# Dense attention on one core: row maxima computed 28 instead of 26 score tiles ahead

## The chip, the cores and the metric

The kernel runs on one core of a Trainium2 chip. The metric is the device time of one execution in microseconds (us); lower is better. The engines are TensorE (PE; its weight loads, PEld, are listed apart), VectorE (DVE), ScalarE (ACT), GpSimd (POOL) and SyncE (SP), which issues the DMAs. Each engine works through its own instructions in order; semaphores tie the engines together.

## What is computed

`x` is (2, 2048, 256). After a first layer norm, two branches read it: a dense attention branch with 16 heads of width 16, and a local attention and feed-forward branch of two layers. The result is `x + s * silu(f)`. The change touches only the dense branch:

```python
qkv = einsum('bnd,ed->bne', x, W_qkv)            # 16 heads of width 16
attn = einsum('bhnd,bhmd->bhnm', q, k) * hd**-0.5
attn = attn + spatial_bias                       # nonzero for tokens 1..256 only
attn = softmax(attn, axis=-1)
out = einsum('bhnm,bhmd->bhnd', attn, v)
out = out @ W_proj.T + b_proj + layernorm(x)
```

## The kernel before

The kernel has three phases: projections and the splitting of q and k into bf16 parts (to about 111 us), the dense attention (111 to 1472 us), and the window branch (to the end). Only the second phase is touched.

**Tiles and groups.** For each of the 16 heads `h` the scores are computed in 128 steps (`STEPS`). A step is one tile of 128 keys by 512 queries. Sixteen steps make a group (`KB` = 16): one batch row and one chunk of 512 queries; a head has 8 groups, groups 0 to 3 for batch row 0 and 4 to 7 for batch row 1. Before a group's first score can be computed, the largest score of each of its 512 queries must be known, because it is subtracted inside the score matmul through two extra rows of `q_aug` (the shift). So the same products are computed once more beforehand, with queries on the partitions (`max_tile`, L1460: four matmuls of 32 columns side by side). Two such tiles are a pair, and eight pairs cover a group: pairs 0 to 7 are group 0, pairs 48 to 55 are group 6. The maxima run `LEAD` tiles ahead of the scores, across the border between heads.

**PE.** Its order is written out in the loop over `turns()` (from L1503). In each step: `scores_to_exp` (L1475), in eight of sixteen steps also `weighted` (probabilities times values, L1492; `PV_PLAN` says where: steps 0, 2, 4, 6, 7, 10, 12, 14 of a group), and in each odd step the two tiles of pair `(step + LEAD) // 2`. `scores_to_exp` waits at a group's first step until the shift rows are stored (`shift_saved`). A pair's tiles go to PSUM banks 4 and 5 or 6 and 7 in turn, so the matmuls of pair t wait until DVE has read pair t-2 (`smax_read`).

**DVE** reads each pair with one reduction (`max_pair`, L1145). In `turns()` order it also does the transposition of a group's shift (`turn_shift`, L1165). It stands behind the first pair of the next group (L1190 to L1193): the shift of group 5 behind pair 48. It waits there for `shift_ready`, and all later reductions are queued behind it.

**POOL** works in the order of `serve_head`. For each group, `split_max` forms four row maxima (L641, each waits for its two pairs), rounds them to bf16 (L645), subtracts (L647, which releases `shift_ready`), waits for DVE's transposition and copies its result into `q_aug` with four instructions (L657). Two things stand between groups. `apply_bias` (L635) multiplies three probability tiles of group 0 and of group 4. `copy_values` (L625) loads the values of a batch row; ahead of the row maxima of group 5 it loads batch row 0 of the next head, for which it waits until the last `weighted` of group 3, at step 71, is done. The last head has no such copy.

**ACT** takes the exponential of each score tile (L919) and stores the sums of each group (L902). **SP** loads `q_aug` and `k_aug` of batch row 0 of the next head after the scores of step 63, and stores the sums.

**The start.** Before step 0, PE computes `LEAD` tiles. DVE reads the first eight pairs, forms the first shift, reads `LEAD // 2 - 8` more pairs (L1182), then sets one row of the bias table (L1185), which releases POOL's first `apply_bias`. The `weighted` of step 10 waits for it (`bias_done`). **The end.** Pair 63 of head 15 is the last, so the last steps have no maxima.

Of the kernel before, what the change touches and what calls it, by code (L numbers as in the profile page):

```python
# [32 lines left out]
KB = N // P  # L33
# [4 lines left out]
SHIFT_ROWS = 2  # L38
CT = 32
AUG = TERM_ROWS + SHIFT_ROWS  # L40
LEAD = KB + 10
TURN = 32
TURNS = P // TURN
PRING = 16
# [43 lines left out]
def build(nc, x, wqkT, wvT, wpT, b_proj, gamma, beta, centers, centersT, wqkv, qk_gain, qk_gain_swapped, rotary,  # L88
# [9 lines left out]
    with ExitStack() as top:  # L98
# [951 lines left out]
        def _(dve):  # L1050
# [88 lines left out]
            def max_pair(h, t):  # L1139

                group, q, half = t // (PAIRS // GROUPS), (t // 2) % QC, t % 2
                if t % (PAIRS // GROUPS) == 0 and h * GROUPS + group >= 2:
                    dve.wait_ge(max_step, 2 * (h * GROUPS + group - 2) + 1)
                dve.wait_ge(smax_ready, h * PAIRS + (t + 1))
                nc.vector.tensor_reduce(pair_max[:, group % 2, q, half:half + 1],  # L1145
                                        banks[:, 4 + 2 * (t % 2):6 + 2 * (t % 2), :],
                                        AX.XY, ALU.max).then_inc(smax_read, 1)
# [33 lines left out]
            nc.vector.tensor_tensor(dmax[:, 4:5], dmax[:, 5:6], dmax[:, 3:4], ALU.mult).then_inc(dist_scale, 1)  # L1181
            for t in range(PAIRS // GROUPS, LEAD // 2):  # L1182
                max_pair(0, t)
            dve.wait_ge(dist_exp, 1)
            nc.vector.memset(bias_exp[0:1, 0, :], 1.0).then_inc(bias_ready, 1)  # L1185
            for h, steps, ends in turns():
                for step in steps:
                    tile = step + LEAD
                    if tile % 2 == 0 or ends and tile > STEPS + 1:
# [222 lines left out]
        def _(pe):  # L1412
# [41 lines left out]
            def max_tile(before, t):  # L1454

                pair, b, q, kq = t // 2, (t // (QC * KB)) % B, (t // (N // BANK)) % KB, t % (N // BANK)
                if t % 2 == 0:
                    pe.wait_ge(smax_read, before + (pair + 1))
                for m in range(0, P, CT):
                    last = nc.tensor.matmul(banks[m:m + CT, 4 + t % 4, :],  # L1460
                                            q_aug[0:TERM_ROWS, b, q * P + m:q * P + m + CT],
                                            k_aug[0:TERM_ROWS, b, kq * BANK:(kq + 1) * BANK], start=True, stop=True)
                if t % 2 == 1:
                    last.then_inc(smax_ready, 1)
# [15 lines left out]
            def weighted(h, group, first, half):  # L1480

                b = group // QC
                if first == 0 and half == 0:
                    pe.wait_ge(acc_saved, h * GROUPS + (group + 1))
                    pe.wait_ge(v_copied, h * 2 + (3 + b))
                    if group % QC == 0:
                        pe.wait_ge(bias_done, h * 6 + (b * 3 + 3))
                if half == 0:
                    pe.wait_ge(prob_ready, h * STEPS + (group * KB + first + 5))
                cols = slice(half * HALF, (half + 1) * HALF)  # L1490
                for g in range(4):
                    last = nc.tensor.matmul(banks[CT * g:CT * g + VW, 3, cols], v_cur[:, b, first + g, :],  # L1492
                                            probs[:, (group * KB + first + g) % PRING, cols],
                                            start=(first == 0 and half == 0), stop=(first == KB - 4),
                                            skip_group_check=True)
                last.then_inc(pv_done, 1)

            nc.tensor.sem_inc(pv_done, 1)
            pe.wait_ge(aug_loaded[0], AUG_LOADS)
            for t in range(LEAD):  # L1500
                max_tile(0, t)
            pe.wait_ge(minus_set, 1)
            for h, steps, ends in turns():  # L1503
                for step in steps:
# [5 lines left out]
                    if group + ago >= 0:  # L1510
                        weighted(h, group + ago, first, half)
                    pair = (step + LEAD) // 2
                    if step % 2 == 1 and not (ends and pair >= PAIRS):
# [318 lines left out]
```

## Time and profile before

| | value |
|---|---|
| median of 3 runs | 2928.17 us (2927.76 to 2928.51) |
| the profiled execution's own time | 2928.38 us |
| its span, first to last instruction | 2926.6 us |
| mean granted TensorE clock | 0.993 |
| PE busy | 2883.0 us (99%) |
| DVE busy | 2336.9 us (80%) |
| ACT busy | 2222.5 us (76%) |
| POOL busy | 1265.3 us (43%) |
| DVE reductions of pairs, L1145 | 1024 of 1214 ns |

The busy time of PE is taken from modelled ends of matmuls, so 99% says that PE nearly always had work, not that it ran at its peak. The idle time before an instruction and what ended it stand in square brackets in the timeline rows. A line number in a row is that of the kernel.

### The profile page before, as it was taken

Reading aid. Unit: us, or ns where it says so; the run is one execution under the profiler, and the core shown is the slowest. Engines: PE = TensorE matmul, PEld = TensorE weight load, DVE = VectorE, ACT = ScalarE, POOL = GpSimd, SP = SyncE. Lnnn points to the kernel's source line nnn. Section 1 sums busy time; section 2 is a strip of 40 time slices with the busy share of each in tenths; the row PEclk is TensorE's granted clock in tenths of the full one; section 3 lists DMA queues with packets and bytes.
Section 4 is the critical chain, followed back from the end, with each engine's and each line's share of the span. In section 5 each row is a group of like instructions: output and inputs, shape, how many; then the busy total and the mean of one; then the engine's idle time right before and its main releaser. Section 6 shows DMA issues by size and latency. Waiting matters only on the chain.

```text
span 2926.6 us, 107289 instructions
## 1 busy us (share of the span) xinstructions
PE 2883.0 (99%) x44160; PEld 2025.9 (69%) x44160; DVE 2336.9 (80%) x4346; ACT 2222.5 (76%) x4251; POOL 1265.3 (43%) x2348
## 2 busy tenths in 40 slices
PE   8899999999999999999999999999999999999998
PEld 4467666655667755767657777777777777777776
DVE  7899999999999999999856776777677677767765
ACT  4599999999999999999966666666666666666664
POOL 5432333333333323332345455555555554555554
PEclk9899999999999999999999999999999999999999
DMA  7631111111111111111121111111111111111110
GB/s 233 211 115 41 49 49 45 43 49 49 41 46 49 49 39 48 49 49 39 44 65 45 36 31 37 40 47 44 30 37 33 47 45 36 31 38 39 47 43 5
DMA packets 157393, 154.78 MB, mean 53 GB/s; under 512 B 17794, under 2 KB 130946, under 8 KB 156930
## 3 DMA queue, kind: packets, MB, share of 16 engines
q1 hardware_dynamic: 156930, 148.15, 16.3%
q8 instruction: 346, 5.67, 0.8%
q14 instruction: 117, 0.96, 0.1%
HBM read 89.37 MB, written 58.72 MB: 51 GB/s over the span
## 4 chain that ended last, share of the span: by engine, by line
PE 95%; DVE 2%; POOL 1%; ACT 1%; issue 1%; SPq 0%; DMA 0%; POOLq 0%; DVEq 0%; ACTq 0%
PE banks L1534 29%; PE banks L1492 15%; PE banks L1460 15%; PE banks L1475 14%; PE banks L1601 4%; PE banks L1549 4%; PE banks L1639 4%; PE banks L1568 3%; PE banks L1616 2%; PE banks L1429 1%; PE banks L1626 1%; DVE pair_max L1145 1%; PE banks L1447 1%; POOL row_max L641 1%; PE banks L1714 0%
## 5 line engine op out<-in xcount | busy, mean ns | idle before, releaser
L1145 DVE TENSOR_REDUCE pair_max<-banks 128x1 f32<-128x1024 f32 x1024 | 1212.4, 1214 | 106.9 <-PE banks L1460 76.4
L919 ACT ACTIVATE probs<-banks 128x512 f32<-128x512 f32 x2048 | 1186.5, 599 | 99.3 <-PE banks L1475 13.1
L1475 PE MATMUL banks<-q_aug,k_aug 98*32 98x512 bf16 x8192 | 845.7, 381 | 0.2
L1460 PE MATMUL banks<-k_aug,q_aug 96*32 96x512 bf16 x8192 | 663.0, 383 | 8.5 <-DVE pair_max L1145 3.8
L1492 PE MATMUL banks<-probs,v_cur 128*32 128x256 f32 x8192 | 655.7, 379 | 2.1 <-POOL probs L635 2.0
L1492 PEld LDWEIGHTS banks<-probs,v_cur 128*32 128x32 f32 x8192 | 319.3, 111 | 144.1 <-issue 2.4
L1460 PEld LDWEIGHTS banks<-k_aug,q_aug 96*32 96x32 bf16 x8192 | 276.8, 97 | 188.2 <-DVE pair_max L1145 60.2
L641 POOL TENSOR_SCALAR row_max<-pair_max 128x1 f32<-128x1 f32 x508 | 139.6, 278 | 611.0 <-DVE pair_max L1145 603.1
L1475 PEld LDWEIGHTS banks<-q_aug,k_aug 98*32 98x32 bf16 x8192 | 287.3, 95 | 150.4 <-ACT probs L919 4.7
L1534 PEld LDWEIGHTS banks<-hnT,w_sb 128*64 128x64 f32 (+1 forms) x5632 | 308.5, 137 | 25.1 <-ACT hnT L998 25.1
L1534 PE MATMUL banks<-hnT,w_sb 128*64 128x128 f32 (+1 forms) x5632 | 323.9, 275 | 0.9 <-ACT hnT L998 0.9
L730 POOL TENSOR_TENSOR norms<-norms,half_power 128x4 f32<-128x4 f32 (+1 forms) x192 | 232.4, 1220 | 181.1 <-DVE norms L1254 181.1
L939 ACT ACTIVATE masked<-banks 128x512 f32<-128x512 f32 x128 | 76.5, 598 | 302.1 <-DVE masked L1222 267.4
L1266 DVE CUSTOM_DVE_ANT_0 masked<-banks,mask,norms 128x256 f32<-128x256 f32 x512 | 212.3, 479 | 43.9 <-PE banks L1601 43.9
L1534 PE MATMUL banks<-wqkv_sb,xT 128*64 128x512 f32 x1024 | 246.2, 602 | 0.0
L1245 DVE TENSOR_REDUCE norms<-masked 128x8 f32<-128x512 f32 x128 | 87.1, 681 | 170.5 <-ACT masked L939 170.5
L657 POOL COPY q_aug<-shift_rows 2x128 bf16<-2x128 bf16 x512 | 146.0, 285 | 161.8 <-DVE shift_rows L1165 138.4
L1534 PE MATMUL banks<-pT,w_sb 128*64 128x128 f32 x3072 | 181.7, 274 | 0.0
L1325 DVE SCALAR_TENSOR_TENSOR pT<-banks,b_sb,pT 128x128 f32<-128x128 f32 (+1 forms) x384 | 113.2, 343 | 74.0 <-PE banks L1534 72.6
L1534 PEld LDWEIGHTS banks<-pT,w_sb 128*64 128x64 f32 x3072 | 169.2, 137 | 3.8
L983 ACT COPY pT<-banks 128x1024 f32<-128x1024 f32 x128 | 123.3, 1015 | 60.9 <-PE banks L1616 60.9
L757 POOL TENSOR_TENSOR oT<-row_sums,one 128x512 f32<-128x512 f32 x64 | 66.5, 1040 | 208.1 <-DVE row_sums L1284 208.1
(143 smaller groups left out, 4020.5 us busy)
## 6 DMA issues: line engine op xcount, KB each, us to landing
acc_scratch<-acc_sb SPq DMA_DIRECT2D x128, 256.0 KB, 2.5
heads_win<-acc_scratch SPq DMA_DIRECT2D x512, 64.0 KB
q_aug<-q_parts SPq DMA_DIRECT2D x192, 64.0 KB, 2.2
k_aug<-k_parts SPq DMA_DIRECT2D x192, 64.0 KB, 2.2
q_parts<-parts SPq DMA_DIRECT2D x16, 384.0 KB, 3.1
k_parts<-parts SPq DMA_DIRECT2D x16, 384.0 KB, 4.1
x_in<-in_x SPq DMA_DIRECT2D x10, 512.0 KB, 4.9
xT_scratch<-xnT SPq DMA_DIRECT2D x8, 512.0 KB, 5.4
```

Source lines behind the costliest of these rows:

```text
L641: last = nc.gpsimd.tensor_scalar(row_max[:, q:q + 1], pair_max[:, group % 2, q, 0:1], pair_max[:, group % 2, q, 1:2], None, ALU.max)
L657: nc.gpsimd.tensor_copy(cols[:, :, g, :], shift_rows[g * TURN:g * TURN + SHIFT_ROWS]).then_inc(shift_saved, 1)
L730: nc.gpsimd.tensor_tensor(norm, norm, half_power[:, 0:last - first], ALU.pow).then_inc(inv_norms, 1)
L919: nc.scalar.activation(probs[:, step % PRING, :], banks[:, ring(h, step), :], ACT.Exp, scale=SCALE).then_inc(prob_ready, 1)
L983: nc.scalar.copy(pT[:, b, first:first + LH // 2].rearrange("p h c (r t) -> p r (h c) t", r=2), banks[:, lanes(b) + first // 2:lanes(b) + f ...
L1145: nc.vector.tensor_reduce(pair_max[:, group % 2, q, half:half + 1], banks[:, 4 + 2 * (t % 2):6 + 2 * (t % 2), :], AX.XY, ALU.max).then_inc ...
L1266: last = nc.vector.tensor_tensor_reduce(masked[:, b, p, :], banks[:, lanes(b) + p // 2, col:col + 2 * WINDOW], mask[:], norms[:, b, head_a ...
L1460: last = nc.tensor.matmul(banks[m:m + CT, 4 + t % 4, :], q_aug[0:TERM_ROWS, b, q * P + m:q * P + m + CT], k_aug[0:TERM_ROWS, b, kq * BANK: ...
L1475: last = nc.tensor.matmul(banks[m:m + CT, ring(h, step), :], k_aug[0:AUG, b, kb * P + m:kb * P + m + CT], q_aug[0:AUG, b, qc * CHUNK:(qc + ...
L1492: last = nc.tensor.matmul(banks[CT * g:CT * g + VW, 3, cols], v_cur[:, b, first + g, :], probs[:, (group * KB + first + g) % PRING, cols], ...
L1534: last = nc.tensor.matmul(out[first:first + size], stationary[:, first:first + size], moving, start=start, stop=stop)
L1549: last = nc.tensor.matmul(out, tokens, weights, start=(f == 0), stop=(f == 1))
```

## The change

One constant is raised:

```diff
-LEAD = KB + 10
+LEAD = KB + 12
```

`LEAD` is 28 instead of 26. PE computes 28 tiles before step 0, and each later pair two steps earlier: the first pair of a group stood in step 7 of a group and now stands in step 5. DVE, POOL, ACT and SP keep their order, but for one pair that DVE reads ahead of the row of the bias table. The last pair of the last head moves from step 101 to step 99.

On DVE, at the start of the second phase, between the first shift's arithmetic and the second shift's transposition:

```order
-L1145 TENSOR_REDUCE pair_max<-banks 128x1 f32<-128x1024 f32 x5
+L1145 TENSOR_REDUCE pair_max<-banks 128x1 f32<-128x1024 f32 x6
 L1185 MEMSET bias_exp 1x256
-L1145 TENSOR_REDUCE pair_max<-banks 128x1 f32<-128x1024 f32 x4
+L1145 TENSOR_REDUCE pair_max<-banks 128x1 f32<-128x1024 f32 x3
```

One reduction moved ahead of the memset; the transposition still follows the ninth of them.

On PE, in head 0, steps 70 to 73 before. L1475 is a step's score tile, L1492 is `weighted`, L1460 a pair of maxima; the second L1492 is the last of group 3, for which POOL's copy of the values waits, and the first L1460 is pair 48:

```order
L1475 MATMUL banks<-q_aug,k_aug 32x512 x4
L1492 MATMUL banks<-probs,v_cur 32x256 x4
L1475 MATMUL banks<-q_aug,k_aug 32x512 x4
L1492 MATMUL banks<-probs,v_cur 32x256 x4
L1460 MATMUL banks<-k_aug,q_aug 32x512 x8
L1475 MATMUL banks<-q_aug,k_aug 32x512 x8
L1460 MATMUL banks<-k_aug,q_aug 32x512 x8
```

The same place in the changed kernel, one row earlier, so that pair 48 is in it, which is the first L1460 and belongs to step 69:

```order
L1460 MATMUL banks<-k_aug,q_aug 32x512 x8
L1475 MATMUL banks<-q_aug,k_aug 32x512 x4
L1492 MATMUL banks<-probs,v_cur 32x256 x4
L1475 MATMUL banks<-q_aug,k_aug 32x512 x4
L1492 MATMUL banks<-probs,v_cur 32x256 x4
L1460 MATMUL banks<-k_aug,q_aug 32x512 x8
L1475 MATMUL banks<-q_aug,k_aug 32x512 x8
L1460 MATMUL banks<-k_aug,q_aug 32x512 x8
```

Pair 48 moved two steps up. The `weighted` of step 71 stood ahead of pair 48 and now stands behind it.

## Rows read from the trace of the kernel before

**Rows 1.** Stretches view: length, busy us of PE, PEld, DVE, ACT, POOL, then clock.

```profile
160.00:1455.00 1295.00, 1293.43 (x23711) 856.27 (x23706) 1188.54 (x1112) 1205.01 (x2099) 403.81 (x1356) 1.00 0.16 50
```

**Rows 2.** DVE timeline, ordinary group: start us, us, what, [idle before <-releaser].

```profile
702.53 1.23 DVE L1145 TENSOR_REDUCE pair_max<-banks 128x1 f32<-128x1024 f32 x1 [0.59 <-PE banks L1460]
...
703.89 8.50 DVE L1145 TENSOR_REDUCE pair_max<-banks 128x1 f32<-128x1024 f32 x7
712.98 1.23 DVE L1145 TENSOR_REDUCE pair_max<-banks 128x1 f32<-128x1024 f32 x1 [0.59 <-PE banks L1460]
```

**Rows 3.** PE timeline, head 7: pair 50, weighted of step 76, pair 51.

```profile
766.64 0.72 PE L1460 MATMUL banks<-k_aug,q_aug 96*32 96x512 bf16 x8
...
767.30 0.72 PE L1492 MATMUL banks<-probs,v_cur 128*32 128x256 f32 x8
...
768.36 0.62 PE L1460 MATMUL banks<-k_aug,q_aug 96*32 96x512 bf16 x8
```

**Rows 4.** Waits between engines, 160 to 1440 us: us in total, times, longest.

```profile
PEld banks L1460 <- DVE pair_max L1145: 44.3, 219, 0.6
POOL v_cur L625 <- PE banks L1492: 33.2, 15, 2.2
...
DVE shift_rows L1165 <- POOL shift L647: 4.9, 15, 0.3
```

**Rows 5.** POOL timeline: copy of values, then the shift of group 5.

```profile
764.87 0.40 POOL L625 COPY v_cur<-v_all 128x256 f32<-128x256 f32 x1 [2.24 <-PE banks L1492]
765.25 1.03 POOL L641 TENSOR_SCALAR row_max<-pair_max 128x1 f32<-128x1 f32 x4
...
766.63 0.21 POOL L647 TENSOR_TENSOR shift<-row_max,shift 128x4 bf16<-128x4 f32 x1
```

**Rows 6.** DVE timeline there: pair 48, transposition, pairs 49 to 55.

```profile
765.32 1.22 DVE L1145 TENSOR_REDUCE pair_max<-banks 128x1 f32<-128x1024 f32 x1 [0.58 <-PE banks L1460]
766.88 0.31 DVE L1165 STREAM_TRANSPOSE shift_rows<-shift 128x128 bf16<-128x128 bf16 x1 [0.34 <-POOL shift L647]
767.12 8.35 DVE L1145 TENSOR_REDUCE pair_max<-banks 128x1 f32<-128x1024 f32 x7
```

**Rows 7.** POOL timeline: end of an ordinary split_max, group 6.

```profile
775.56 0.28 POOL L641 TENSOR_SCALAR row_max<-pair_max 128x1 f32<-128x1 f32 x1 [2.33 <-DVE pair_max L1145]
...
776.20 0.21 POOL L647 TENSOR_TENSOR shift<-row_max,shift 128x4 bf16<-128x4 f32 x1
```

**Rows 8.** POOL timeline, group 0 of a head: apply_bias, last row maximum.

```profile
718.65 2.12 POOL L635 TENSOR_TENSOR probs<-probs,bias_exp 128x256 f32<-128x256 f32 x3 [2.85 <-ACT probs L919]
...
722.94 0.28 POOL L641 TENSOR_SCALAR row_max<-pair_max 128x1 f32<-128x1 f32 x1 [1.41 <-DVE pair_max L1145]
```

**Rows 9.** SP timeline: issue of six loads of q_aug, next head.

```profile
759.33 4.06 SPq L433 DMA_DIRECT2D q_aug<-q_parts  x6
```

**Rows 10.** DVE timeline at the start: five pairs, the bias table row.

```profile
122.19 5.97 DVE L1145 TENSOR_REDUCE pair_max<-banks 128x1 f32<-128x1024 f32 x5
128.16 0.27 DVE L1185 MEMSET bias_exp<- 1x256 f32 x1
```

**Rows 11.** POOL timeline at the start: an all-reduce, then apply_bias.

```profile
116.67 0.38 POOL L619 PARTITION_ALL_REDUCE dmax<-dmax  x1 [5.93 <-issue]
...
133.82 2.08 POOL L635 TENSOR_TENSOR probs<-probs,bias_exp 128x256 f32<-128x256 f32 x3 [10.56 <-ACT probs L919]
```

**Rows 12.** PE timeline at the start: step 10 weighted, pair 19.

```profile
136.16 0.64 PE L1492 MATMUL banks<-probs,v_cur 128*32 128x256 f32 x8 [1.98 <-POOL probs L635]
...
139.03 0.61 PE L1460 MATMUL banks<-k_aug,q_aug 96*32 96x512 bf16 x8 [0.72 <-DVE pair_max L1145]
```

**Rows 13.** ACT timeline, end of the phase, no maxima on PE.

```profile
1457.93 7.97 ACT L919 ACTIVATE probs<-banks 128x512 f32<-128x512 f32 x16
```

**Rows 14.** Stretches view: the start after step 7, and a stretch behind the phase.

```profile
132.00:142.00 10.00, 7.30 (x132) 3.40 (x124) 6.80 (x7) 6.26 (x12) 5.63 (x16) 1.00 0.01 2
...
1480.30:1483.50 3.20, 3.20 (x12) 1.04 (x12) 0.71 (x2) 1.07 (x2) 1.99 (x2) 0.50 0.60 155
```

## The prediction

> **What bounds the kernel now.** I read the stretches view first. From 160 to 1455 us PE is busy for 1293.4 of 1295 us at full clock; DVE has 1188.5 and ACT 1205.0 us of work [rows 1]. Then DVE's timeline of an ordinary group: the same reduction comes back after 712.98 - 702.53 = 10.45 us [rows 2]. In a group PE has 16 score tiles and 16 tiles of maxima of four matmuls each, and eight `weighted`, which the trace shows as eight matmuls each, as many as a pair [rows 3]. So a group is 16 + 16 + 2 x 8 = 48 slots of 0.218 us, one behind the other. PE's own work is the bound, and neither its amount nor the length of a slot changes. A gain can only come from a stall of PE that goes, a loss only from one that comes.
>
> The stalls are few. The waits view has one that belongs to a place in each head: 15 times POOL's copy of values waits for PE (33.2 us), and 15 times DVE's transposition waits for POOL's shift, 4.9 us in all [rows 4]. It is the shift of group 5, in every head but the last.
>
> **That place, before.** POOL's copy waits for the `weighted` of step 71 and starts at 764.87. Four row maxima, the cast and the subtraction follow, and the shift is ready at 766.63 + 0.21 = 766.84 [rows 5]. DVE had read pair 48 from 765.32 on, then stood 0.34 us, transposed at 766.88 and began with pair 49 at 767.12 [rows 6]. PE may start pair 51 only when pair 49 has been read: it did at 768.36, which is 1.24 us behind the start of that reduction [rows 3]. Without a wait, pair 51 would have come six slots behind pair 50: 766.64 + 6 x 0.218 = 767.95 [rows 3]. PE lost 0.41 us here; 4.9 us over 15 heads, 0.33 each, say the same for the others [rows 4].
>
> **The same place, after.** Nothing that sets the moment of the shift moves: the copy waits for the same `weighted` of step 71, at the same place of PE's order of scores. So shift at 766.84, transposition at 766.88, pair 49's reduction at 767.12, pair 51 not before 768.36 (in the clock of before). What moves is pair 51: it belongs to step 75 instead of 77. Two scores and a `weighted` (1 + 1 + 2 slots) no longer stand ahead of it, nor does pair 48, which is now done before the `weighted` of step 71 (2 slots). Counted from that `weighted`, PE comes to it six slots earlier, at 766.64. It stands 768.36 - 766.64 = **1.72 us**, with the scores of step 76 and all else queued behind. The loss grows by 6 x 0.218 = 1.31 us for each head. DVE waits with nothing to do from the end of pair 48's reduction, about 765.32 - 0.58 = 764.74 [rows 6], to 766.88.
>
> Is it given back, or does more follow? PE has no reserve to give back [rows 1]. Behind the stall DVE reads pairs 49 to 55 in 8.35 us; with the last one 1.22 long this is (8.35 - 1.22) / 6 = 1.19 us for each [rows 6]. Pair 52 then may start at 767.12 + 1.19 + 1.24 = 769.55, and PE reaches it at 768.36 + 1.31 = 769.67. No second stall, by 0.12 us only; after that DVE gains 0.12 us with each pair. Sum: 15 x 1.31 = **+19.6 us**.
>
> **The ordinary groups.** The shift is ready at 776.20 + 0.21 = 776.41 [rows 7], 0.94 us behind the end of the group's last reduction at 767.12 + 8.35 = 775.47 [rows 6]. After the change one reduction of 1.22 us stands between that end and the transposition, so the shift is there about 0.28 us early, and DVE doesn't wait. The transposition (0.2 us of DVE: 703.89 against 702.53 + 1.23, with the overlap of about 0.1) falls into the 0.59 us in which DVE waits for PE anyway [rows 2]. That gives DVE slack and PE nothing: 0. Were the cover of 0.28 us gone, DVE would wait by what is missing, and PE would stand only from some 0.2 us on, the slack that is left of the 0.59.
>
> In group 0 of a head `apply_bias` stands ahead of the row maxima. It ends at 718.65 + 2.12 = 720.77; four maxima, cast and subtraction take 766.84 - 765.25 = 1.59 us [rows 5], so the shift is ready at 722.36. DVE would start its transposition when the reduction of the pair of step 5 is done, close to 722.9, since that is what POOL's last row maximum waited for at 722.94 [rows 8]. Cover: 0.5 us. At 0. Should it be gone by some tenths, PE still has a slot or two before it needs the pair.
>
> The first maxima of the next head need its `q_aug` at step 101 instead of 103. The six loads are issued in 4.06 us [rows 9], the six of `k_aug` behind them, from step 64 on; 37 steps of 0.65 us are 24 us. At 0.
>
> **The start.** One more pair is read ahead of the bias table's row. DVE reads these at 5.97 / 5 = 1.19 us [rows 10], so the row is set at 129.4 instead of 128.2. POOL's first `apply_bias` started at 133.82, 5.4 us behind the end of that memset at 128.43, though step 0's probabilities were there long before [rows 10, 11]. There is a like gap ahead of the all-reduce: 5.93 us with no releaser [rows 11]. If the 5.4 us run from the semaphore on, `apply_bias` moves by 1.2 us and with it the `weighted` of step 10, on which PE already stands 1.98 us [rows 12]; if they run from somewhere earlier, it stays at 133.82. I take +1.2, because the gap has the length of the all-reduce's; the other end is 0.
>
> The Trainium skill, "GPSIMD Engine Reference", section "Instruction dispatch", says that the first call into freshly loaded code pays about 6 us after its wait, with no visible instruction. The rows agree with 5.9 and 5.4 us. By that rule the term would be the +1.2 already taken from the rows.
>
> PE's longer lead of about 1.2 us (one more pair at DVE's rate) is not added: PE is waiting at step 10 in either case. From there on pair 19 is held by the second shift at 139.03 [rows 12], as before, plus the 1.2; it is now issued in step 11, so the scores run two steps behind it.
>
> **The end.** For that, two more steps have no maxima. These run at ACT's pace there, 7.97 / 16 = 0.50 us a step [rows 13]: **+1.0 us**. The pairs themselves are no more than before.
>
> **Sum:** 19.6 + 1.2 + 0 + 1.0 = 21.8 us. The profiled execution took 2928.38 us for a span of 2926.6; its new span would be 2948.4 and its time 2950.2. The median lies 0.2 us lower: 2928.17 + 21.8 = **2950.0 us**.
>
> **Rivals.**
> 1. *The clock falls at each new stall.* PE now stands 1.7 us in the middle of dense work, 15 times. A stretch of 3.2 us behind the phase was granted half the clock, after PE had idled [rows 14]. If each stall brought one such stretch, half of 3.2 us of PE's time would be lost each time: 15 x 1.6 = 24 us more, 2974. Against it: at the start PE stood 1.98 and 0.72 us within 4 us [rows 12], and 132 to 142 us was granted 1.00 [rows 14]. Chance 0.05. The Trainium skill, "TensorE: Matmul & The Clock Gate", section "HAM oscillation — how this bites in real kernels", tells of a kernel whose PE waited for each tile and fell to the lower rate every time; that rule would give this rival's time, and the start of this trace does not bear it out for a stall of this length.
> 2. *The stall does not grow.* DVE waits longer, but PE is not held, for instance since the reads of pairs 49 and 50 catch up before PE comes. Then only start and end are left, +2.2 us: 2930.4. For it: 0.41 us is all that PE loses now. Against it: PE was held at exactly that pair, and needs it six slots earlier. Chance 0.05.
> 3. *Faster: PE's waits for DVE in ordinary groups are real time.* PE's weight loads wait 44.3 us for DVE, 219 times [rows 4], near two in each group; the transposition's move starts the reduction of a group's second pair 0.2 us earlier and could end them. It decides from 21.8 / 127 = 0.17 us a group on. With all 44.3 us gone: 2928.2 + 21.8 - 44.3 = 2905.7. Against it: a group lasts 48 even slots with those waits in it, so they lie under the matmuls ahead. Chance 0.02.
>
> That the change does not do what it says is no rival: the order shows pair 48 ahead of the `weighted` of step 71.
>
> **How the numbers follow.** Forecast 0.86, rival 1 0.05, rival 2 0.05, rival 3 0.02, something unseen 0.02. The range takes in the unknown of the start (-1.2), a stall by 0.1 to 0.3 us off in each head (up to 4.5), and a second short stall at pair 52, whose cover is 0.12 us: 2943 to 2957. About 0.2% (6 us) is what a measurement of this kernel can tell from no change. Faster 0.02, same 0.05, slower 0.93.
>
> **What would show it.** Right: DVE's transposition waits for POOL's shift 15 times for some 2.1 us, over 30 us in the waits view; PE stands ahead of pair 51 about 1.7 us in each head, in step 75; an ordinary group still lasts 10.45 us, with DVE's idle time ahead of the pair of step 7 down from 0.59 to near 0.4; `apply_bias` first starts near 135.0; the phase ends near 1494. Wrong: ordinary groups that change in length, a granted clock below 1 in the phase after 140 us, or the transposition waiting in ordinary groups too, which would cost some tenths of a microsecond 112 times.

## The result and the profile after

The median is 2949.82 us (2949.60 to 2952.09, 6 runs) against 2928.25 us (2927.76 to 2928.90, 6 runs): 21.6 us or 0.75% slower. The ratio is 1.0075, 95% interval 1.0062 to 1.0088. The forecast was 2950.0. The profiled execution took 2949.7 us for a span of 2947.9, at a mean granted clock of 0.993 as before.

The stretches view of the changed kernel (length, busy us of PE, PEld, DVE, ACT, POOL, then clock), to be held against [rows 1]; below it, three stretches of the start:

```profile
160.00:1455.00 1295.00, 1274.05 (x23356) 843.46 (x23352) 1192.38 (x1095) 1187.66 (x2068) 397.50 (x1335) 1.00 0.16 49
132.60:139.40 6.80, 3.89 (x68) 1.45 (x64) 3.40 (x4) 3.31 (x7) 5.11 (x15) 1.00 0.01 2
139.50:142.80 3.30, 3.30 (x40) 1.29 (x34) 2.50 (x3) 1.79 (x3) 0.44 (x2) 0.50 0.00 0
142.90:160.00 17.10, 17.10 (x324) 9.06 (x316) 15.20 (x16) 15.62 (x28) 3.98 (x16) 1.00 0.05 19
```

PE's busy time in the same 1295 us fell from 1293.4 to 1274.1. Its idle time, 1.6 us before, is 21 us now. At the start, behind two stands of PE, the clock was granted at half rate (1.2 GHz instead of 2.4) from 139.4 to 142.8 us; the trace of the kernel before has full rate there [rows 14].

The waits view, 160 to 1440 us, answers [rows 4]:

```profile
POOL v_cur L625 <- PE banks L1492: 33.2, 15, 2.2
DVE shift_rows L1165 <- POOL shift L647: 31.0, 15, 2.1
PEld banks L1460 <- DVE pair_max L1145: 28.4, 15, 1.9
ACT probs L919 <- PE banks L1475: 24.6, 15, 1.7
PE banks L1460 <- DVE pair_max L1145: 20.9, 15, 1.4
```

POOL's wait for the `weighted` of step 71 is unchanged, 33.2 us in 15. DVE's wait for the shift went from 4.9 to 31.0 us, again 15 times and so in no ordinary group. PE's weight loads wait for DVE 15 times instead of 219. The place itself in head 7, in the timelines of POOL, DVE and PE; they answer [rows 5], [rows 6] and [rows 3]:

```profile
776.64 0.40 POOL L625 COPY v_cur<-v_all 128x256 f32<-128x256 f32 x1 [2.20 <-PE banks L1492]
...
778.41 0.21 POOL L647 TENSOR_TENSOR shift<-row_max,shift 128x4 bf16<-128x4 f32 x1
```

```profile
775.37 1.23 DVE L1145 TENSOR_REDUCE pair_max<-banks 128x1 f32<-128x1024 f32 x1
778.65 0.31 DVE L1165 STREAM_TRANSPOSE shift_rows<-shift 128x128 bf16<-128x128 bf16 x1 [2.06 <-POOL shift L647]
778.89 8.37 DVE L1145 TENSOR_REDUCE pair_max<-banks 128x1 f32<-128x1024 f32 x7
```

```profile
778.31 0.43 PE L1475 MATMUL banks<-q_aug,k_aug 98*32 98x512 bf16 x4
780.13 0.61 PE L1460 MATMUL banks<-k_aug,q_aug 96*32 96x512 bf16 x8 [1.39 <-DVE pair_max L1145]
```

The chain from the copy to the shift has kept its length, 778.62 - 776.64 = 1.98 us. Pair 48 is read from 775.37 on, before the copy that the shift waits for has begun; DVE then stands 2.06 us. Pair 49 begins to be read at 778.89 and PE starts pair 51 at 780.13, 1.24 us later as before. A slot behind the score at 778.31 would have been 778.53: a stall of 1.60 us. The 1.39 us in the row are less, because modelled ends of matmuls reach into the gap.

An ordinary group, timeline of DVE, answers [rows 2]:

```profile
808.33 1.23 DVE L1145 TENSOR_REDUCE pair_max<-banks 128x1 f32<-128x1024 f32 x1 [0.15 <-PE banks L1460]
809.47 0.30 DVE L1165 STREAM_TRANSPOSE shift_rows<-shift 128x128 bf16<-128x128 bf16 x1
810.00 2.36 DVE L1145 TENSOR_REDUCE pair_max<-banks 128x1 f32<-128x1024 f32 x2 [0.23 <-PE banks L1460]
```

The transposition waits for nothing. Of the 0.59 us for which DVE waited for PE once a group, 0.15 are left ahead of the pair of step 5 and 0.23 ahead of that of step 7. The start, timelines of POOL and PE, answers [rows 11] and [rows 12]; the end, timeline of ACT, answers [rows 13]:

```profile
133.48 2.09 POOL L635 TENSOR_TENSOR probs<-probs,bias_exp 128x256 f32<-128x256 f32 x3 [10.53 <-ACT probs L919]
```

```profile
135.83 0.64 PE L1492 MATMUL banks<-probs,v_cur 128*32 128x256 f32 x8 [0.81 <-ACT probs L919]
...
138.71 0.62 PE L1460 MATMUL banks<-k_aug,q_aug 96*32 96x512 bf16 x8 [2.02 <-DVE pair_max L1145]
```

```profile
1479.44 7.99 ACT L919 ACTIVATE probs<-banks 128x512 f32<-128x512 f32 x16
```

In this execution the second phase began 0.30 us earlier (first maxima at 110.37 instead of 110.67). With that taken off, `apply_bias` and pair 19 stand where they stood before, though the bias table's row was set 1.1 us later (done at 129.26 instead of 128.43).

### The profile page after: what moved, and what is told of

Same layout as the page of the kernel before. It is cut to its first block, busy times and chain, and to the rows that moved or that the text cites. A ratio compares the mean times of both kernels' runs of the same rounds, so it can differ in the third digit from the quotient of the medians.

```text
span 2947.9 us, 107289 instructions
## 1 busy us (share of the span) xinstructions
PE 2884.4 (98%) x44160; PEld 2028.4 (69%) x44160; DVE 2362.8 (80%) x4346; ACT 2222.8 (75%) x4251; POOL 1267.9 (43%) x2348
## 4 chain that ended last, share of the span: by engine, by line
PE 93%; DVE 4%; POOL 1%; issue 1%; ACT 1%; SPq 0%; DMA 0%; POOLq 0%; DVEq 0%; ACTq 0%
PE banks L1534 29%; PE banks L1492 15%; PE banks L1460 15%; PE banks L1475 15%; PE banks L1601 4%; PE banks L1549 4%; PE banks L1639 4%; PE banks L1568 3%; PE banks L1616 2%; DVE pair_max L1145 1%; PE banks L1626 1%; DVE xn L1091 1%; POOL row_max L641 1%; DVE xn L1081 0%; DVE rest L1098 0%
## 5 line engine op out<-in xcount | busy, mean ns | idle before, releaser
L1145 DVE TENSOR_REDUCE pair_max<-banks 128x1 f32<-128x1024 f32 x1024 | 1226.5, 1221 | 79.5 <-PE banks L1460 40.6
L1475 PE MATMUL banks<-q_aug,k_aug 98*32 98x512 bf16 x8192 | 846.2, 382 | 0.2
L1460 PE MATMUL banks<-k_aug,q_aug 96*32 96x512 bf16 x8192 | 663.6, 383 | 30.1 <-DVE pair_max L1145 26.2
L1492 PE MATMUL banks<-probs,v_cur 128*32 128x256 f32 x8192 | 656.4, 380 | 1.0 <-ACT probs L919 0.8
L1460 PEld LDWEIGHTS banks<-k_aug,q_aug 96*32 96x32 bf16 x8192 | 285.6, 98 | 203.1 <-DVE pair_max L1145 45.8
L1492 PEld LDWEIGHTS banks<-probs,v_cur 128*32 128x32 f32 x8192 | 318.1, 111 | 145.8 <-issue 1.8
L1475 PEld LDWEIGHTS banks<-q_aug,k_aug 98*32 98x32 bf16 x8192 | 288.1, 95 | 152.9 <-ACT probs L919 4.9
```

What stands on the lines that cost most here:

```text
L1460: last = nc.tensor.matmul(banks[m:m + CT, 4 + t % 4, :], q_aug[0:TERM_ROWS, b, q * P + m:q * P + m + CT], k_aug[0:TERM_ROWS, b, kq * BANK: ...
L1475: last = nc.tensor.matmul(banks[m:m + CT, ring(h, step), :], k_aug[0:AUG, b, kb * P + m:kb * P + m + CT], q_aug[0:AUG, b, qc * CHUNK:(qc + ...
```

## The experiments

Theory A is that of the forecast: POOL makes the shift of group 5 only behind a copy that waits for the `weighted` of step 71; DVE, in order, waits for that shift and leaves pair 49 unread; PE, in order, waits at pair 51. The earlier PE reaches pair 51, the longer it stands. Rival B: the longer lead costs by itself. What is said of stalls and of the clock is read from one profiled execution of each kernel; the times are medians. The single runs of one kernel spread by 3 us to either side in the first two series below, also those of the kernel before, more than in the result above. Stalls named below are read from the starts of PE's matmuls, less one slot of 0.218 us.

### Taking the cause away: POOL's other order, and a second buffer

```diff
                 apply_bias(h, 1)
+                split_max(h, QC + 1)
                 if next_head is not None:
                     pool.wait_ge(pv_done, h * PVH + (PVH // 2 + 1))
                     copy_values(next_head, 0)
-                for group in range(QC + 1, GROUPS + (next_head is not None)):
+                for group in range(QC + 2, GROUPS + (next_head is not None)):
```

> LEAD 28, and on POOL the row maxima and the shift of group 5 stand ahead of the copy of the next head's values instead of behind it. Theory A (DVE waits for a shift that POOL can only make after the weighted of step 71, and PE waits for DVE): the 15 stalls of 1.64 us ahead of pair 51 vanish, 24.7 us in all, so 2949.8 - 24.7 = 2925.1, which is also below the kernel before. Rival B (the earlier maxima as such cost time, by their place between the scores, whatever POOL does): stays near 2949.8. Rival C (DVE waits anyway, because apply_bias of group 4 is late too): the stall shrinks to some tenths, 2928 to 2935.

Measured: 2925.71 us, ratio to the kernel before 0.9994 (0.9985 to 1.0003), before in the same series 2927.50. The 15 stalls are gone, all of them, so neither rival B nor rival C of the expectation holds. The waits view, 160 to 1440 us, has only five rows left; neither DVE's wait for the shift nor PE's for DVE is among them (the line numbers are one higher, by the added line):

```profile
POOL row_max L641 <- DVE pair_max L1146: 600.0, 336, 2.3
POOL probs L635 <- ACT probs L920: 142.0, 31, 4.6
POOL q_aug L657 <- DVE shift_rows L1166: 87.5, 123, 1.1
DVE pair_max L1146 <- PE banks L1461: 35.8, 173, 0.2
DVE pair_max L1146 <- POOL row_max L641: 0.5, 1, 0.5
```

```diff
-        v_cur = sb("v_cur", [P, B, KB, VW], F32)
+        v_cur = sb("v_cur", [P, 2, B, KB, VW], F32)
...
-                nc.gpsimd.tensor_copy(v_cur[:, b, :, 0:HD],
+                nc.gpsimd.tensor_copy(v_cur[:, h % 2, b, :, 0:HD],
...
-                    pool.wait_ge(pv_done, h * PVH + (PVH // 2 + 1))
+                    pool.wait_ge(pv_done, h * PVH + 1)
...
-                    last = nc.tensor.matmul(banks[CT * g:CT * g + VW, 3, cols], v_cur[:, b, first + g, :],
+                    last = nc.tensor.matmul(banks[CT * g:CT * g + VW, 3, cols], v_cur[:, h % 2, b, first + g, :],
```

> LEAD 28, POOL's order as it was, but the values of a head go to one of two buffers in turn, so that the copy ahead of group 5 need not wait for the weighted of step 71. Theory A with the wait as the cause: 2925.1 as with the other order. If it were POOL's work ahead of the row maxima (the copy of 0.4 us itself) and not its wait: near 2949.8, at most 15 x 0.4 = 6 us less.

Measured: 2927.36 us, ratio 1.0001 (0.9992 to 1.0011). No stall at group 5 in the trace. POOL's copy still stands ahead of the row maxima of group 5 here, but it runs at once, at 180.45, behind `apply_bias`:

```profile
179.76 0.73 POOL L635 TENSOR_TENSOR probs<-probs,bias_exp 1x256 f32<-1x256 f32 x1
180.45 0.39 POOL L625 COPY v_cur<-v_all 128x256 f32<-128x256 f32 x1
180.83 1.02 POOL L641 TENSOR_SCALAR row_max<-pair_max 128x1 f32<-128x1 f32 x4
```

So it is the wait for PE inside POOL's order, not POOL's work. Rival B falls as the cause of the 20 us. The longer lead is not quite free, though: with POOL's other order, LEAD 26 (below) came 3.6 us under the kernel before and LEAD 28 only 1.8, and the 1.0 us of the end is part of that difference, which the spread of the runs hardly resolves.

### The lead alone: the transposition left in step 7

```diff
-                    if tile % 2 == 0 or ends and tile > STEPS + 1:
+                    if tile % 2 == 0 or ends and tile > STEPS + 3:
...
-                    if tile // 2 % (PAIRS // GROUPS) == 0:
+                    if tile // 2 % (PAIRS // GROUPS) == 1:
```

> LEAD 28, POOL's order as it was, but the transposition stands behind the second pair of the next group (pair 49 in step 71 for group 5) and so in the same step as in the kernel before. Theory A: the pair that is held is 52 in step 77, and the stall is again that of before, 0.33 us a head: 2949.8 - 15 x 1.31 = 2930.2. Rival B (the maxima's lead itself costs): stays near 2949.8.

Measured: 2927.65 us, ratio 1.0002 (0.9992 to 1.0011), below the 2930.2 expected. The stalls came out as expected: 15, of 5.1 us in all against 4.9 before, now at pair 52 in step 77. Two rows of the waits view, 160 to 1440 us, show it:

```profile
PEld banks L1460 <- DVE pair_max L1145: 9.2, 15, 0.6
DVE shift_rows L1165 <- POOL shift L647: 6.2, 15, 0.4
```

Of the 2.5 us between expectation and result, 1.7 would be the half-rate stretch at the start, which this trace lacks while the changed kernel's has it, and 0.7 the lower level of the kernel before in this series.

### More of the cause: a later copy, and a longer lead

```diff
-                    pool.wait_ge(pv_done, h * PVH + (PVH // 2 + 1))
+                    pool.wait_ge(pv_done, h * PVH + (PVH // 2 + 2))
```

> LEAD 28, and the copy waits for one weighted more, the first of group 4 in step 74, which stands 9 slots of 0.218 us behind that of step 71. Theory A: each stall grows by 1.96 us to 3.6 us, 15 x 1.96 = 29.4 us more, 2979.2, while the clock stays at full rate. If PE's clock falls at a stall of this length, each adds up to 1.7 us more: to 3004. Rival B: no change from 2949.8.

Measured: 3005.24 us, ratio 1.0264 (1.0248 to 1.0279). It was the higher of the two times expected. The stalls are 3.55 to 3.70 us, 54.1 in all, which is 29.4 more than in the changed kernel; and the clock fell after each of the 15. The timeline of PE and the stretches view, at one of them:

```profile
187.54 0.62 PE L1460 MATMUL banks<-k_aug,q_aug 96*32 96x512 bf16 x8 [3.35 <-DVE pair_max L1145]
```

```profile
189.10:192.40 3.30, 3.30 (x36) 1.42 (x32) 1.94 (x3) 1.77 (x3) 0.28 (x1) 0.50 0.50 160
192.50:277.70 85.20, 81.83 (x1508) 53.05 (x1504) 76.36 (x71) 76.23 (x133) 25.90 (x87) 1.00 0.17 49
```

Each such stretch lasts 3.4 us in this trace, and PE gets half of its work done in it: 15 x 1.7 = 25.5 us. 2949.8 + 29.4 + 25.5 = 3004.7, measured 3005.2. (At the start this trace has 6.8 us at half rate instead of 3.4; the sum leaves these 1.7 us out.) The 15 stretches begin 88.7 us apart each time: the heads repeat one another and are not 15 independent trials.

```diff
-LEAD = KB + 10
+LEAD = KB + 14
```

> LEAD 30: the transposition stands behind the pair of step 3, pair 51 in step 73. Theory A: each stall grows by 6 slots once more, 1.64 + 1.31 = 2.95 us: 2949.8 + 19.6 + 1.0 = 2970.4, and up to 0.7 us in group 0 of each head, where apply_bias makes the shift late too, of which PE's slack takes most: up to 2980. At the start apply_bias stands again 10.5 us behind POOL's last copy (near 133.8) if that gap runs from the copies, and near 136 if it runs from the bias table's row.

Measured: 2995.36 us, ratio 1.0232 (1.0215 to 1.0248), 15 us above the upper end of what was expected. In the waits view, 160 to 1440 us, DVE waits for the shift 29 times now:

```profile
DVE shift_rows L1165 <- POOL shift L647: 61.6, 29, 3.4
PEld banks L1460 <- DVE pair_max L1145: 57.2, 32, 3.2
```

15 of the stalls are those of group 5 and measure 2.90 to 3.05 us, the 1.31 us more that were expected. Another 15 of 0.3 us stand in group 0, and one in the last head, where `apply_bias` now makes the shift late. What the expectation left out is the clock: 12 of the long stalls were followed by a half-rate stretch. 2949.8 + 19.6 + 1.0 + 15 x 0.3 + 12 x 1.7 = 2995.3.

### Where the clock begins to fall

The edit of the late copy, with LEAD 26:

> LEAD 26, and the copy waits for one weighted more, the first of group 4 in step 74. Theory A: each of the 15 stalls grows from 0.33 by 9 slots of 0.218 us (1.96 us) to 2.29 us: 2928 + 29.4 = 2957.5 if the granted clock stays at full rate as it did at 1.64 us, and up to 15 x 1.7 = 25 us more, 2983, if it falls as it did at 3.0 and 3.6 us. The number of half-rate stretches in the trace tells which, and may lie between.

Measured: 2967.14 us, ratio 1.0128 (1.0111 to 1.0145). The 15 stalls are 2.25 to 2.37 us. The clock fell after 5 of them, in every third head; the stretches view at the first, and the long full-rate stretch behind it with two more such stalls in it:

```profile
273.00:276.30 3.30, 3.30 (x36) 1.30 (x32) 2.27 (x2) 1.67 (x4) 0.28 (x1) 0.50 0.02 5
276.50:532.30 255.80, 249.54 (x4580) 168.81 (x4572) 228.85 (x214) 232.33 (x406) 78.89 (x263) 1.00 0.14 46
```

2957.5 + 5 x 1.7 = 2966.0, without the start, where this trace has 6.8 us at half rate behind step 10 and the kernel before has none. So a stall of 1.6 us cost itself alone in 15 of 15 cases here, one of 2.3 us brought a half-rate stretch in 5 of 15, one of 3.0 us in 12, one of 3.6 us in all 15. Each count is of one trace; the single runs of the kernel with 2.3 us spread from 2964.0 to 2970.0, so other executions can have had fewer or more.

### The other direction: less lead, and the best of POOL's order

The diff is again one number, `LEAD = KB + 8`.

> LEAD 24, nothing else: the transposition stands behind the pair of step 9 and pair 51 in step 79. Theory A: 1.31 us more room for each stall of 0.33 us, which vanishes (-4.9); two steps fewer without maxima at the end (-1.0); the start is held by apply_bias as before: 2922.3. If the extra lead or its lack mattered by itself in each group, the time would move by more than these, for instance if DVE, now with its transposition behind two close pairs, held PE in ordinary groups: 112 times some tenths of a microsecond, 2930 to 2960.

Measured: 2924.01 us, ratio 0.9987 (0.9978 to 0.9996), before in this series 2927.87. No stall is left in the 16 heads, and ordinary groups hold. POOL's copy waits as ever, and DVE no longer for the shift; the first rows of the waits view, 160 to 1440 us:

```profile
POOL row_max L641 <- DVE pair_max L1145: 679.7, 321, 2.8
DVE pair_max L1145 <- PE banks L1460: 63.4, 123, 0.5
POOL q_aug L657 <- DVE shift_rows L1165: 57.3, 123, 0.6
POOL probs L635 <- ACT probs L919: 55.2, 31, 1.8
POOL v_cur L625 <- PE banks L1492: 33.3, 15, 2.2
```

POOL's order changed at LEAD 26, and at LEAD 24:

> LEAD 26 as before, with POOL's other order (shift of group 5 ahead of the copy of values). Theory A: the 15 stalls of 0.33 us of the kernel before vanish: 2928.2 - 4.9 = 2923.3. If the stall of before has another cause: 2928.2.

> LEAD 24 with POOL's other order. Theory A: nothing is left to remove at group 5, so the same as LEAD 24 alone, 2922.3 (within 1 us).

Measured: 2924.26 us, ratio 0.9989 (0.9980 to 0.9998), and 2923.72 us, ratio 0.9984 (0.9975 to 0.9994). The three kernels, LEAD 24 alone and these two, are 3.6 to 4.2 us below the kernel before and 1 to 2 us above what was expected. Their traces have no stall at group 5, so the heads gave the 4.9 us; at the start, though, PE stands 3.0 to 3.6 us ahead of the `weighted` of step 10, and a half-rate stretch of 3.4 or 6.8 us follows, which the kernel before lacks.

### The start

What does POOL wait for ahead of the first `apply_bias`? The edit puts a tiny multiply of the same kind as `apply_bias` right behind the all-reduce:

```diff
+            pool.wait_ge(dist_red, 2)
+            nc.gpsimd.tensor_tensor(dmax[:, 6:7], dmax[:, 1:2], dmax[:, 1:2], ALU.mult).then_inc(first_mult, 1)
             copy_values(0, 0)
```

(The line that declares the semaphore `first_mult` is left out here.)

> LEAD 28, and one tiny multiply on POOL (128x1, its result is not used) right behind the all-reduce, ahead of the copies of the first values and shift. Theory D (the 10.5 us ahead of the first apply_bias run from the switch of POOL's code, which the trace shows 0.05 us behind the copies, and not from the bias table's row): the tiny multiply itself starts late, 6 to 10.5 us behind the all-reduce, at 122.5 to 127.5, and the first apply_bias then starts as soon as the table's row and step 0 are there, near 129.5 to 131 instead of 133.5; PE no longer stands ahead of the weighted of step 10. Theory E (the gap belongs to the wait for the row): apply_bias still starts 4 to 5 us behind the row. Time: within 3 us of 2949.8, since the first shift is saved later by what the multiply costs.

Measured: 2943.49 us (2 runs), ratio 1.0051 (1.0031 to 1.0071), 6.3 us below the changed kernel and 3 us below the lower end of what was expected. Timeline of POOL:

```profile
117.08 0.38 POOL L620 PARTITION_ALL_REDUCE dmax<-dmax  x1 [5.89 <-issue]
124.36 0.18 POOL L678 TENSOR_TENSOR dmax<-dmax 128x1 f32<-128x1 f32 x1 [6.90 <-issue]
...
130.51 2.09 POOL L636 TENSOR_TENSOR probs<-probs,bias_exp 128x256 f32<-128x256 f32 x3 [4.21 <-ACT probs L922]
```

The time went to the multiply, 6.90 us with no releaser, and `apply_bias` starts 0.50 us behind the bias table's row, which was done at 130.01. Theory D holds and not E: the time belongs to POOL's return to other code after the all-reduce, and not to the wait for the row. The other runs say the same. POOL's switch of its code stands in the trace 0.05 us behind the last copy; from there to `apply_bias` it took 10.1 to 11.5 us in all nine experiments without the early multiply and in both kernels, while `apply_bias` stood anything from 2.7 (LEAD 30) to 6.8 us (LEAD 24) behind the bias table's row. PE then stands neither at step 10 nor at pair 19, and no half-rate stretch follows: the changed kernel's trace has 1.0 and 2.2 us there and 1.7 us through the clock, 4.9 of the 6.3 us; 0.7 more are the lower level of the kernel before in this series, and the last 0.7 lie within the spread of the runs. Why the same return took 6.9 us here and 10.5 otherwise is open. One rival stands in the traces and no run tests it: SP issues the load of the next phase's weights (3 MB) shortly ahead of POOL's switch. In the changed kernel the load landed 10.3 us behind its issue, at 131.9, with the DMA engines full meanwhile, and `apply_bias` came at 133.48; the early multiply had its 6.9 us mostly ahead of that load. Against it speaks that the 6.0 us ahead of the all-reduce began under full DMA engines too (110.4 to 114.0 us, busy share 1.00). An SP row and a stretch of the changed kernel, then a stretch of the run with the early multiply; the last two numbers of a stretch are the DMA engines' busy share and GB/s:

```profile
121.57 0.38 SPq L478 DMA_DIRECT2D wqkv_sb<-in_wqkv  x1
124.00:131.00 7.00, 6.62 (x64) 1.91 (x64) 6.45 (x7) 2.17 (x4) 0.00 (x0) 0.50 0.99 410
117.50:123.50 6.00, 4.29 (x36) 0.55 (x32) 5.77 (x13) 1.18 (x1) 0.00 (x0) 0.50 0.52 126
```

### Both remedies

POOL's other order together with the early multiply, at LEAD 26 and 24:

> LEAD 26, POOL's other order (shift of group 5 ahead of the copy of values) and the tiny multiply behind the all-reduce. Theory A and D together: no stall at group 5 (-4.9), none ahead of step 10 and of the second shift (-3.1) and no half-rate stretch after them (up to -3.4 against the run with the order alone): 2918 to 2921. If the start's gain were lost again further on: 2924.3 as with the order alone.

> The same with LEAD 24. Theory A and D: 1.0 us less at the end, but here PE comes to step 0 at 125.1, ahead of the first shift's copies, which the multiply puts back to about 126.3; so 0 to 1 us from the one with LEAD 26, 2918 to 2921.

Measured: 2918.96 us, ratio 0.9967 (0.9956 to 0.9979), and 2918.98 us, ratio 0.9966 (0.9952 to 0.9979), before in this series 2928.04. Both beat both kernels, by 9 us the one before. In both traces, no stall of PE over 0.3 us is left between step 0 and the last maxima, the early multiply took 7.4 and 6.6 us, and `apply_bias` starts 0.5 and 0.6 us behind the bias table's row.

## Why the prediction was right, and where it was not

**The stall of each head: right.** The term was 15 x 1.31 = 19.6 us. Measured are 15 stalls of 24.7 us in all against 4.9, so 19.8. The forecast said 1.72 for head 7 and 1.60 was measured, since the other heads' 0.33 rather than this head's 0.41 is the usual start; the difference of six slots is what held. Its cause is shown by taking away the wait (2925.7 and 2927.4 us in all) and its size by the stall at four leads, 0 at LEAD 24, 0.33 at 26, 1.64 at 28 and 3.0 at 30, and by the later copy, 2.3 at LEAD 26 and 3.6 at 28.

**No second stall at pair 52: right.** None is in the trace, with 0.12 us of cover.

**Ordinary groups at nothing: right.** DVE's wait for the shift stands 15 times, in no ordinary group. The idle time of DVE ahead of the pair of step 7 fell to 0.23 us and not to near 0.4: the transposition takes the 0.2 us that were forecast (809.77 against 809.56), and another 0.15 us of waiting now lie ahead of the pair of step 5. Together they are 0.38. That changed nothing for PE. Rival 3, that PE's weight loads waited in real time, is refuted: 204 of 219 such waits vanished and no time came back.

**The start: wrong by its term.** `apply_bias` was to move by 1.2 us, to 135.0; it stayed, at 133.48. The step that failed is that the gap begins at the semaphore of the bias table's row; it begins at the switch of POOL's code, and the bound of 0 was the right end. The forecast had taken a gap of 5.4 us from the row for a second case of the 5.9 us ahead of the all-reduce, and their likeness was chance. The Trainium skill, "GPSIMD Engine Reference", section "Instruction dispatch", gives about 6 us for the first call after the wait is taken off. The all-reduce agrees with 5.9 us, and the early multiply comes near with 6.9. Ahead of `apply_bias` it does not hold: behind the row the time was anything from 2.7 to 6.8 us, and 10.1 to 11.5 us from the switch; there the measurement decides.

**The clock: right in the heads, missed at the start.** After 1.6 us of standing the clock did not fall, in 15 of 15. But at the start PE stands twice, 1.0 us ahead of step 10 and 2.2 us ahead of pair 19, since pair 19 now comes two steps earlier, and in this trace a half-rate stretch followed, 1.7 us. I had priced rival 1 for the heads only and let the start's waiting cover everything there. So two errors, 1.2 us too much and 1.7 us left out, nearly cancelled, and that the sum of 21.8 came within 0.2 us of the measured 21.6 is luck. Rival 1's mechanism is real: with stalls 0.7 us longer it came in every third head of the trace.

**The end: right.** From the last tile of the last pair to the last `weighted` it took 1471.22 - 1455.62 = 15.60 us, and now 1492.75 - 1476.16 = 16.59: 1.0 us more.

The terms added up for the two profiled spans: 19.8 + 0 + 1.7 + 1.0 is 22.5, less the 0.3 us by which this execution came earlier to the phase, against 21.3 measured. Of the 0.9 us left over, 0.24 are a single stall of the kernel before in head 10 that this one lacks; the rest is spread over the slots and not explained.

## What to carry to other kernels

Where an engine works in order, a wait costs what is queued behind it, so ask for each wait how early the engines behind it now arrive: running work further ahead made PE arrive earlier at a buffer whose release did not move. One such wait (POOL's for PE) reached PE again by way of DVE, and its sign was the same count, 15, in three rows of the waits view. Look at the work that stands ahead of the shared result in the slowest-moving queue (here a copy for the next head), and move that before giving the fast engines more lead. A stall of 1.6 us cost itself; one of 2.3 us or more could cost 1.7 us on top through the clock.

## What the runs showed of the hardware

- The granted clock after one isolated stand of PE in dense work: 1.6 us left it at full rate (0 of 15 in the changed kernel, 0 of 15 again with the early multiply), 2.3 us brought a half-rate stretch of 3.4 us in 5 of 15 cases, 3.0 us in 12, 3.6 us in 15. Each cost 1.7 us. Each count comes from one trace.
- At the start, two stands close together were followed by one in the changed kernel (1.0 and 2.2 us) and in the two LEAD 28 kernels without the cause (0.9 and 2.2, 1.25 and 2.1 us), but not in the kernel before (2.15 and 0.93 us) nor with the transposition in step 7 (1.7 and 0.9 us). Whether the second stand alone would have done it is not shown.
- POOL's return from the all-reduce to multiplying took 10.1 to 11.5 us from the switch of its code when copies stood ahead of the switch, and 6.6 to 7.4 us when the multiply came at once; the copies themselves did not wait for it (in the changed kernel the first started at 116.68, before the all-reduce of 116.42 had ended). A tiny operation placed early took the return out of PE's way; the time fell by 6.3 us at LEAD 28, of which the traces show 4.9.
